# Layer norms that keep their value in PSUM, and a silu clip that reads z from PSUM before the exponent

## The reference, cut to what matters

```python
def _ssm(x, ...):
    ...                                         # scan h = h * da + dbx, y = sum of h * c
    y = ys.transpose(1, 0, 2) + xt * Dv
    return _layernorm(y, g, be)                 # (y - mu) / sqrt(var + 1e-5) * g + be

y3 = ssm(fx3) + flip(ssm(flip(fx3)))            # 64 positions
y2 = ssm(fx2) + flip(ssm(flip(fx2))) + up2(y3)  # 256 positions
y1 = ssm(fx1) + flip(ssm(flip(fx1))) + up2(y2)  # 1024 positions
out = y1 * silu(z)
return conv1x1(out, out_w, out_b)
```

## Time and profile before

| what | value |
|---|---|
| median of 3 runs | 4518.45 us (4516.85 to 4525.16) |
| the profiled execution: its time | 4519.6 us |
| its span | 4517.8 us |
| TensorE's granted clock, mean | 0.809 of full |
| DVE busy | 3744.5 us, 83% |
| POOL busy | 3355.6 us, 74% |
| PE busy | 3112.7 us, 69% |
| ACT busy | 2556.6 us, 57% |

### The profile page before, as it was taken

The page is one execution under the profiler, slowest core; times in us unless marked ns, Lnnn a source line. Parts: engine busy times, 40 slices in busy tenths (PEclk is TensorE's granted clock), DMA queues, the critical chain, the costliest instruction groups (busy, mean ns, idle before and its releaser), DMA issues.

```text
span 4517.8 us, 51130 instructions
## 1 busy us (share of the span) xinstructions
PE 3112.7 (69%) x11852; PEld 1453.0 (32%) x11852; DVE 3744.5 (83%) x4199; ACT 2556.6 (57%) x6006; POOL 3355.6 (74%) x1908
## 2 busy tenths in 40 slices
PE   6967767767766777777777776777776677776511
PEld 3433333233333333333233333333333233332200
DVE  2178888888888888888888888888888888898787
ACT  4465565656565565666556555564666556565432
POOL 0079596886959789595886958689596887969697
PEclk8988887888887888887888877788888888888755
DMA  1035353453534445253443534445353444535444
GB/s 39 1 137 193 108 182 134 155 179 123 194 122 159 140 161 195 101 192 117 165 163 133 200 105 170 143 151 192 103 192 131 153 158 146 189 108 181 147 161 157
DMA packets 187259, 663.93 MB, mean 147 GB/s; under 512 B 22736, under 2 KB 24672, under 8 KB 186976
## 3 DMA queue, kind: packets, MB, share of 16 engines
q1 hardware_dynamic: 186976, 661.47, 42.8%
HBM read 639.76 MB, written 21.63 MB: 146 GB/s over the span
## 4 chain that ended last, share of the span: by engine, by line
POOL 26%; issue 25%; DVE 21%; PE 12%; ACT 10%; DMA 4%; DVEq 1%; POOLq 1%; SPq 0%; ACTq 0%
POOL bx L1345 11%; POOL y L1373 7%; DVE h L581 6%; ACT diag L1088 5%; POOL h L1368 5%; DMA bb<-bc_rows 4%; PE pconv L824 4%; DVE slot_c L572 4%; DVE o L637 2%; POOL bx L1348 2%; PE pm L850 2%; DVE o L632 2%; DVE rs L528 1%; PE pm L841 1%; DVE rs L520 1%
## 5 line engine op out<-in xcount | busy, mean ns | idle before, releaser
L824 PE MATMUL pconv<-pad,diag 128*128 128x512 f16 x8064 | 2065.0, 414 | 178.6 <-DVE xn L506 111.3
L1373 POOL TENSOR_TENSOR y<-y,h 128x1024 f32<-128x1024 f32 (+2 forms) x672 | 1338.1, 1991 | 330.5 <-DVE h L581 307.7
L1203 ACT ACTIVATE slot_b<-delta,nega 128x512 f32<-128x512 f32 (+1 forms) x1280 | 807.3, 641 | 1169.4 <-DVE slot_c L572 1167.3
L824 PEld LDWEIGHTS pconv<-pad,diag 128*128 128x128 f16 x8064 | 831.1, 105 | 1394.3 <-issue 462.6
L1345 POOL TENSOR_TENSOR bx<-bb,u 128x1024 f32<-128x1024 f32 x512 | 1233.1, 2408 | 0.0
L572 DVE TENSOR_TENSOR_SCAN slot_c<-slot_b,bx 128x512 f32<-128x512 f32 (+1 forms) x1024 | 954.2, 956 | 281.1 <-POOL bx L1345 238.9
L581 DVE TENSOR_TENSOR h<-slot_c,cb 128x512 f32<-128x512 f32 x1280 | 860.3, 673 | 36.6 <-POOL y L1373 36.6
L572 DVE TENSOR_TENSOR_SCAN slot_c<-slot_b,slot_c,bx 128x512 f32<-128x512 f32 x512 | 663.7, 1296 | 74.5 <-ACT slot_b L1203 18.5
L1313 POOL TENSOR_TENSOR delta<-delta,rs 128x512 f32<-128x512 f32 (+1 forms) x96 | 111.8, 1165 | 457.4 <-DVE rs L530 457.4
L1368 POOL TENSOR_TENSOR h<-h 128x512 f32<-128x512 f32 (+3 forms) x384 | 361.9, 942 | 98.3 <-DVE h L551 80.7
L1088 ACT ACTIVATE diag<-id,chi 128x128 f16<-128x128 f16 x1344 | 426.6, 387 | 10.2 <-PE pconv L824 9.6
(11 more groups left out here) (166 smaller groups left out, 3817.5 us busy)
## 6 DMA issues: line engine op xcount, KB each, us to landing
bb<-bc_rows SPq DMA_DIRECT2D x592, 512.0 KB, 4.4
cb<-bc_rows SPq DMA_DIRECT2D x592, 512.0 KB, 4.3
xr<-in_x SPq DMA_DIRECT2D x16, 1024.0 KB, 5.0
out<-ob SPq DMA_DIRECT2D x16, 1024.0 KB
bc_rows<-rows SPq DMA_DIRECT2D x64, 64.0 KB, 1.6
w<-in_w SPq DMA_DIRECT2D x2, 256.0 KB
wc<-in_wc SPq DMA_DIRECT2D x2, 256.0 KB
bc_rows<-rows SPq DMA_DIRECT2D x16, 32.0 KB, 1.5
```

The source lines that it names most:

```text
L824: ins = nc.tensor.matmul(bank(pconv, k), w, pad[:, t, part, rows:rows + 16, dx:dx + W], start=first and m == 0, stop=last and m == 2)
L1203: ins = nc.scalar.activation(slot_b[:, o:o + w], delta[:, so + c:so + c + w], ACT.Exp, scale=nega[:, st, n0 + n:n0 + n + 1])
L1373: pool.tensor_tensor(yv, yv, src[:, 0] if len(src.shape) == 3 else src, ALU.add).then_inc(q_y.sem, 1)
```

## The change

Three things change.

1. `norm` on DVE multiplies in place in PSUM (`t_` is now the first bank of `norm_psum`), and the steps behind it read and write there. For norms 0 and 1 the order becomes: scale and shift the second direction into SBUF (`x`, in rs), then scale the first direction and add `x`; norm 1's sum stays in PSUM, and `up_add` gets a third operand, `base`, so that it reads the PSUM value and writes o2 in SBUF. For norms 2 and 3 the scale and shift goes PSUM to PSUM, and `up_add` writes o1. For norms 4 and 5 the scaled sum goes to PSUM and the product with sz to o1.
2. Since the PSUM bank is in use until the norm's last step, PE's next users of pm wait for that step (`n_o`) and no longer for the first product (`n_t`): chunk 4 in unit 13, the centring of norms 1 to 3, and `project_f` in unit 36. `output` exchanges slot_b and slot_c between its halves, and its wait for the last norm's first product goes.
3. silu's clip goes from unit 6 to the end of DVE's bridge: it reads z from pm (1024 columns), adds the bias, takes the maximum with -41 and writes o1. ACT's exponential in unit 5 reads o1 in place of sz. `chunk(i, 2)` on PE waits for the clip too.

```diff
@@ -531,8 +531,8 @@
 
-                dve.wait_ge(b_z.sem, b_z.at(i, 2))
-                nc.vector.tensor_scalar(o1[:, :], o1[:, :], 1e18, None, ALU.min).then_inc(z_clip.sem, 1)
+                dve.wait_ge(b_z.sem, b_z.at(i, 1))
+                nc.vector.tensor_scalar(o1[:, :], pm[:, :], v_inz, -41.0, ALU.add, ALU.max).then_inc(z_clip.sem, 1)
 
@@ -600,14 +600,14 @@
 
-            def up_add(dst, src, side):
-
-                dv = dst.rearrange("p (r s c) -> p r s c", s=2, c=2 * side)
+            def up_add(dst, base, src, side):
+
+                dv, bv = (v.rearrange("p (r s c) -> p r s c", s=2, c=2 * side) for v in (dst, base))
                 sv = src.rearrange("p (r c) -> p r c", c=side)
...
                 for s in range(2):
-                    d = dv[:, :, s, :].rearrange("p r (c e) -> p r c e", e=2)
-                    ins = nc.vector.tensor_tensor(d, d, sv[:, :, :, None].to_broadcast([P, rows, side, 2]), ALU.add)
+                    d, b = (v[:, :, s, :].rearrange("p r (c e) -> p r c e", e=2) for v in (dv, bv))
+                    ins = nc.vector.tensor_tensor(d, b, sv[:, :, :, None].to_broadcast([P, rows, side, 2]), ALU.add)
                 return ins
@@ -620,27 +620,25 @@
                 step.n = STEPS[k]
-                t_ = norm_sbuf(k)[1][:, 0:cols]
+                t_, x = norm_psum(k)[0][:, 0:cols], norm_sbuf(k)[1][:, 0:n]
                 dve.wait_ge(n_rs.sem, n_rs.at(i, k + 1))
-                ins = nc.vector.tensor_tensor(t_, norm_psum(k)[0][:, 0:cols], norm_sbuf(k)[2][:, 0:cols], ALU.mult)
-                ins.then_inc(n_t.sem, 1)
+                nc.vector.tensor_tensor(t_, t_, norm_sbuf(k)[2][:, 0:cols], ALU.mult).then_inc(n_t.sem, 1)
                 dve.wait_ge(n_t.sem, n_t.at(i, k + 1))
                 if k < 2:
-                    o = (o3, o2)[k]
-                    step(nc.vector.tensor_tensor(o[:, :], t_[:, 0:n], t_[:, n:2 * n], ALU.add))
                     p = 2 - k
-                    step(nc.vector.tensor_scalar(o[:, :], o[:, :], v_g[:, p:p + 1], bes[:, p:p + 1], ALU.mult, ALU.add))
+                    o = (o3[:, :], t_[:, 0:n])[k]
+                    step(nc.vector.tensor_scalar(x, t_[:, n:2 * n], v_g[:, p:p + 1], bes[:, p:p + 1], ALU.mult, ALU.add))
+                    step(nc.vector.scalar_tensor_tensor(o, t_[:, 0:n], v_g[:, p:p + 1], x, ALU.mult, ALU.add))
                     if k == 1:
-                        step(up_add(o2[:, :], o3[:, :], 8))
+                        step(up_add(o2[:, :], o, o3[:, :], 8))
                 elif d == 0:
-                    o = o1[:, c0:c0 + n]
-                    step(nc.vector.tensor_scalar(o, t_, v_g[:, 0:1], bes[:, 0:1], ALU.mult, ALU.add))
+                    step(nc.vector.tensor_scalar(t_, t_, v_g[:, 0:1], bes[:, 0:1], ALU.mult, ALU.add))
                     hh = c0 // HALF
-                    step(up_add(o, o2[:, hh * 128:hh * 128 + 128], 16))
+                    step(up_add(o1[:, c0:c0 + n], t_, o2[:, hh * 128:hh * 128 + 128], 16))
                 else:
                     o = o1[:, c0:c0 + n]
-                    step(nc.vector.scalar_tensor_tensor(o, t_, v_g[:, 1:2], o, ALU.mult, ALU.add))
-                    nc.vector.tensor_tensor(o, o, sz[:, c0:c0 + n], ALU.mult).then_inc(b_g.sem, 1)
+                    step(nc.vector.scalar_tensor_tensor(t_, t_, v_g[:, 1:2], o, ALU.mult, ALU.add))
+                    nc.vector.tensor_tensor(o, t_, sz[:, c0:c0 + n], ALU.mult).then_inc(b_g.sem, 1)
                 assert step.n == STEPS[k + 1]
@@ -648,7 +646,7 @@
                     dve.wait_ge(b_out.sem, b_out.at(i, 2 * hh + t + 1))
-                    src = bank((slot_c, slot_b)[hh], t)
+                    src = bank((slot_b, slot_c)[hh], t)
                     ins = nc.vector.scalar_tensor_tensor(ob[:, t, hh * HALF:(hh + 1) * HALF], src, v_out[:, t:t + 1],
@@ -678,6 +676,8 @@
                 some(4, 5)
+                if j is not None:
+                    silu_clip(j)
 
@@ -688,8 +688,6 @@
                         chunk_last(i, CHUNK_LAST[k])
-                    if k == 6:
-                        silu_clip(i)
                     if k in NORM_DVE:
@@ -854,8 +852,9 @@
                     pe.wait_ge(b_z.sem, b_z.at(i, 1))
+                    pe.wait_ge(z_clip.sem, z_clip.at(i, 1))
                 if c == 4:
-                    pe.wait_ge(n_t.sem, n_t.at(i, 2))
+                    pe.wait_ge(n_o.sem, n_o.at(i, STEPS[2]))
                 if c == 0:
@@ -871,7 +870,7 @@
                 elif k < 4:
-                    pe.wait_ge(n_t.sem, n_t.at(i, k))
+                    pe.wait_ge(n_o.sem, n_o.at(i, STEPS[k]))
                 pe.wait_ge(q_y.sem, q_y.at(i, NORM_NEEDS[k]))
@@ -886,10 +885,8 @@
                 pe.wait_ge(b_g.sem, b_g.at(i, hh + 1))
-                if hh == 0:
-                    pe.wait_ge(n_t.sem, n_t.at(i, NN))
                 for t in range(CT):
-                    nc.tensor.matmul(bank((slot_c, slot_b)[hh], t), wo[:, t * P:(t + 1) * P], o1[:, hh * HALF:(hh + 1) * HALF],
+                    nc.tensor.matmul(bank((slot_b, slot_c)[hh], t), wo[:, t * P:(t + 1) * P], o1[:, hh * HALF:(hh + 1) * HALF],
                                      start=True, stop=True).then_inc(b_out.sem, 1)
@@ -943,7 +940,7 @@
                         if i is not None:
-                            pe.wait_ge(n_t.sem, n_t.at(i, 4))
+                            pe.wait_ge(n_o.sem, n_o.at(i, STEPS[4]))
                         if m is not None:
@@ -1169,11 +1166,11 @@
             def silu_exp(i):
-                act.wait_ge(b_z.sem, b_z.at(i, 1))
-                nc.scalar.activation(o1[:, :], sz[:, :], ACT.Exp, scale=-1.0).then_inc(b_z.sem, 1)
+                act.wait_ge(z_clip.sem, z_clip.at(i, 1))
+                nc.scalar.activation(o1[:, :], o1[:, :], ACT.Exp, scale=-1.0).then_inc(b_z.sem, 1)
 
             def silu_end(i):
-                act.wait_ge(z_clip.sem, z_clip.at(i, 1))
+                act.wait_ge(b_z.sem, b_z.at(i, 2))
                 nc.scalar.activation(o1[:, :], o1[:, :], ACT.Ln, bias=1.0).then_inc(z_ln.sem, 1)
```

## The result

The changed kernel takes **4335.2 us** (median of 3 runs, 4333.3 to 4338.19) where the kernel before takes 4518.45; the ratio is 0.959, with a 95% interval of 0.957 to 0.961. The forecast was 4340, with a range of 4295 to 4425. The profiled execution has a span of 4336.4 us and took 4338.2.

What follows compares the result with a forecast made beforehand. POOL was taken to set the pace, bearing DVE 2.52 us late. Per image 4.45 (norms 0, 1) plus 6.9 (norms 2, 3) make 11.35 us, times 16 is 182 off 4519.6: 4340 us, range 4295 to 4425.

Steps and rivals of the forecast that it cites:

- What stops a pass: On DVE, SBUF-fed scale-and-shift passes and adds of two SBUF operands wait for POOL's running instruction; PSUM-fed passes don't.
- Norms 2 and 3: DVE's norms in units 30 and 33: 3.35 us back behind norm 2, 3.05 plus some 0.5 behind norm 3; together 6.9.
- Norms 0 and 1: DVE's first two norms: lateness stays under POOL's cover of 2.52 us, so POOL's idle 1.51 and 2.94 go: 4.45 us.
- the first rival: DVE's chunk 4 and 5 passes, units 14 to 16, meet new waits for POOL: 75 us, 4415 us; chance 0.12.
- my signs of being wrong: Passes to PSUM at 1 us and more; L520, L528 and L530 longer; PE as what L506 waits for.
- Prices: Norm passes on DVE: product 0.68 us, scale and shift 0.68 (0.41 in norm 1), up-adds 410 ns each.
- Writing to PSUM: DVE's elementwise writes to PSUM cost little; taken as nothing, with ends of -0.05 and 0.68 us a pass.
- the upper end of 0.68: Extra 0.68 us per pass of 512 columns from reading and writing one PSUM bank in turns: 5.2 us an image.
- its rival: PSUM read and written in turns in DVE's passes: 83 us off the gain, 4421 us; chance 0.07.
- The clip: Leaving unit 6 gives nothing; at DVE's bridge end its 1.2 to 1.3 us hide under 1.9 of cover; bare, 20 in all.
- PE: PE's added waits, up to 2.3, 0.5, 1.4 and 1.5 us, have only taps behind them; some 3 us stay ahead of L506.

Runs made afterwards that it cites:

- experiment 3: Changed kernel, but for norms 2 and 3 the product goes to SBUF and the scale and shift reads it there and writes PSUM: 4338.9 us.
- Experiment 4: Changed kernel repeated: 4339.0 us; with three extra DVE passes behind norm 2's product 4377.0, behind norm 3's 4372.1, in unit 24 4330.5.
- experiment 6: Changed kernel with SP's DMAs of chunk 4 and 5 rows issued behind the same unit's loads of bb and cb: 4360.9 us, ratio 0.965.
- experiment 5: Changed kernel with three clips in a row at the end of DVE's bridge, two into unread buffers: 4337.2 us, against 4339.0 with one.
- experiment 1: Changed kernel with the old clip put back: 4356.4 us; kernel before with the new clip alone: 4520.2 us.
- experiment 2: Changed kernel with the value of norms 2 and 3 back in SBUF: 4449.7 us; with that of norms 0 and 1: 4452.2 us.

## Why the prediction was right

**What stops a pass: right, and sharper now.** The long durations were waits for POOL, as the earlier trace rows said, and they are gone in every norm pass. My wording ("passes from SBUF") was too wide: experiment 3 shows that with a single source the destination has to be in SBUF too.

**Norms 2 and 3: right in size (6.80 against 6.9), wrong in the reason for a part.** I took norm 2's gain from POOL's idle time (3.35) and added 0.5 for the smaller lateness. Experiment 4 shows that POOL doesn't enter: DVE never waits for another engine from norm 2 to the sum, and what counts is what DVE itself saves, 3.92 and 2.88 us. That my 3.85 came so near to 3.92 is luck: 3.35 us is POOL's idle time in the image of the rows and in three others, and in the remaining twelve it is 2.9 to 3.0. In the earlier trace rows this could be read: from 1792.21 to 1803.64 there are 11.43 us, three units of 3.82, with no room for a wait.

**Norms 0 and 1: right in the sum (4.15 against 4.45), not in the parts.** The two misses nearly cancel, which is luck too. Between norm 0 and norm 1 it is as behind norm 2: DVE waits for no other engine, so all 2.33 that it saves show, and not POOL's 1.51. Behind norm 1 I had 2.94, and 1.82 came. DVE saves 3.0 there (5.62 us from the product to the next scan before, 2.62 now), but two things take some back, both to be seen in the changed kernel's rows of experiment 6. L520 waits 0.56 us for ACT, because chunk 4 on PE now waits for the norm's end, and the next L520 takes 2.2 us beside POOL where it took 1.43 before. That is the first rival in small: waits for POOL that move on. It had a chance of 0.12 at 75 us; some 0.8 us an image, 12 us, is what came of it. A longer L520 was among my signs of being wrong, and in the mean over its passes of 512 columns it did go from 1083 to 1187 ns.

**Prices.** Up-add 0.42 a pass (said 0.41), product 0.69 (0.68), scaled sum 0.49 (0.48). The scale and shift was too cheap: 0.82 and not 0.68, 0.54 and not 0.41 for 256 columns. Experiment 4 names it: 691 ns with two constants, 741 with one operand of one value per partition, 801 with two, all three from PSUM to SBUF. I had priced it from L625, which has none.

**Writing to PSUM: right.** The product went from 677 ns to SBUF to 686 to PSUM, the scaled sum of L642 from 752 to 759 (L640, whose source moved to PSUM too). 7 to 9 ns a pass; the upper end of 0.68, and its rival, are out. The product of norms 4 and 5 (L641), now with one source in PSUM, takes 691 to 692 ns, and took 692 from SBUF alone (L643 in the earlier trace rows). The Trainium skill (VectorE: DVE Perf Modes, the section on the TRN2 errata) asks for 62 cycles more with a PSUM source; the trace doesn't show them.

**The clip: hidden, as said, and too pessimistic on unit 6.** 1.27 us long, and experiment 5 shows that three of them are still covered. What I priced at nothing in unit 6 gave back some: 0.3 us an image in the trace, where POOL was slower beside the old clip, and 10 to 21 us in the time, most of which stays open (experiment 1).

**PE: covered, with a thinner margin.** PE's last taps ahead of the sum and its waits for the clip (timeline, waits; changed kernel):

```profile
1736.42 3.78 PE L822 MATMUL pconv<-pad,diag 128*128 128x512 f16 x12
```

```profile
PE pm L863 <- DVE o L535: 31.9, 13, 2.5
```

The taps end at 1740.20, 3.9 us ahead of the sum at 1744.14 (said: some 3 stay). PE's wait for the clip is 2.45 us each (31.9 us in 13 waits), said 2.3, and costs nothing: in experiment 5 the clip that PE waits for came behind two more, and the time stayed. But the waits aren't free where something hangs on PE, and there I was wrong to see only taps behind them: chunk 4's products, through ACT, feed DVE's L520. That costs 0.56 us in unit 14, and 2.38 when the norm is slow (experiment 2).

## What to carry to other kernels

Here a DVE instruction whose duration varied or didn't fit its width was waiting inside. Where you see one, look at what POOL runs beside it, and take the instruction off SBUF on one side before changing anything else: a source in PSUM, or, with a single source, the destination. (Two sources in SBUF with the destination in PSUM wasn't tried.) To price a saving on an engine, first ask from where to where it is never idle: within such a stretch every microsecond counts, and another engine's idle time is the wrong measure even where it gives the same sum. When a stretch hangs on one result, put everything on that engine that isn't needed for it behind it. And before closing an idle gap of one engine, look at what the other gets done in it.

## What the runs showed of the hardware that I had not expected

- A DVE pass with two operands of one value per partition (scale and bias) takes 801 ns for 512 columns from PSUM to SBUF (819 to PSUM), with one 741, with constants 691: 50 to 60 ns for each.
- One source in SBUF and the destination in PSUM is enough to keep clear of POOL (814 ns; from PSUM to PSUM 819).
- The idle time of 2.37 us between DVE's last instruction of a loop's body and the first of the next isn't a fixed cost: work put at the end that waits for nothing fills it. With one clip of 1.27 us 0.98 us were left, with three none.
- A pass of 64 columns with both sources in SBUF stood for 5.13 us beside POOL, in some images and not in others (0.54). Taking away POOL's wait of 1.15 us for a load made such a pass 2.3 us longer, and with it moving two DMAs out of a load's way lost 29 us instead of gaining.
- 2.06 us of idle time on PE were followed by products at nearly half speed (2.07 us against 1.12; mean granted clock 0.67 in the one shown) in three images, and it cost nothing, since the pass that waited for them was held up for as long by POOL.
